# Cross-attention and a mixture of experts on one core: the expert loop of TensorE turned and lengthened, the context projection in fp32, two powers made one

## The chip, the core and the metric

The kernel runs on one core of a Trainium2 chip. The metric is device time in microseconds of one execution; the median of several executions counts. Engines: PE (TensorE), DVE (VectorE), ACT (ScalarE), POOL (GpSimd) and SP (which only issues transfers here). PE's clock is granted at one of two levels, 1.2 or 2.4 GHz (0.5 and 1.0 in the profile).

## The reference, cut to what matters

Sixteen batches (tiles) of 128 x 256. Attention part, then a mixture of 16 experts with two shared ones:

```python
def attention(x, ctx):                      # per batch: 128 x 256 each
    xn = layernorm(x)                       # over the 256 columns
    th = theta_w @ ctx + theta_b            # 64 x 256
    ph = phi_w @ xn + phi_b                 # 64 x 256
    p = softmax(th.T @ ph)                  # 256 x 256
    t = (p @ (g_w @ xn + g_b).T).T          # 64 x 256
    h = relu((t - mean(t)) * rsqrt(var(t) + 1e-5) * gamma + beta)   # mean and var of all of t
    return x + out_w @ h + out_b + ctx

def ffn(x):                                 # 2048 tokens of 256
    xt = layernorm(x)
    scores = softmax(xt @ Wg.T)             # 16 experts, 4 groups, top 2 groups, top 4 experts
    y = sum(weight[e] * (silu(xt @ W1[e].T) * (xt @ W3[e].T)) @ W2[e].T for e in chosen)
    return x + y + (silu(xt @ Ws1.T) * (xt @ Ws3.T)) @ Ws2.T
```

Inner width of an expert: 176 (2 x 176 for the shared ones).

## The kernel before, in words

Each engine runs its own program; semaphores carry every dependence, and each program's order is written out by hand.

**Attention part.** A software pipeline of `STEPS` = 21 steps. In step s each engine calls, in the order of its `step` function, the parts of tiles s, s-1, ... by lag (`tile(s, v, lag, part)`); `group(...)` parts run once for four tiles (routing: v - 8, 9 and 10; the counting matmuls and what waits for them fall into steps 10, 14 and 18). POOL's pipeline is longer (`POOL_LAG` = 11): it scatters tile s-11 into the experts' rows by four indirect DMAs a step, from step 11 on. Of the order, this matters here:

- ACT: `exps` (lag 2), `context_high` (lag 0, L499: fp16 copy of the context), copies, `theta_phi` (L458), ..., `normalised_high` (lag 0, L493: fp16 copy of the normalised x), `weights_high` (one expert's weights to fp16 a step).
- DVE: ..., `latent_var` (lag 3, L899), `stats2`, `latent_centre`, `aggr2` (lag 4, L928: `bn_aggr` of the second norm), `normalise` (lag 0, L843: first norm), `latent_out` (lag 3, L910: writes `hpre`), `weights_low` (L945), `normalise2` (lag 4, L934: writes `xn2`).
- POOL: `low` (lag 5, L1341), `context_low` (lag 1, L1315: what fp16 leaves of the context), `normalised_low` (L1335), two scatters (L1351), `latent_rstd` (lag 3, L1319: add epsilon, power -0.5, over one column), `add_context` (L1313), `rstd2` (lag 4, L1327: the same for the second norm, one column), two scatters.
- PE: `theta` (L600) and `phi` (L605) multiply high and low halves by `wparts`, three fp16 matmuls of 256 columns; `scores` (L618) uses fp32.

Matrices are kept as fp16 pairs (high, low) and three products give fp32 precision; `WS` = 64 scales the weights.

**Shared experts, first part.** `shared_units`: 11 of 16 tiles, two units a tile, while POOL finishes the scatters and DVE the last routing group.

**Expert part.** `NT` = 80 tiles of 128 rows. `expert_pipeline` runs 8 steps, then a loop of `BODY` = 8 steps a turn (nine turns), then `lags` = 3 steps. In step s:

- PE (`estep`, L778): loads addresses of four tiles' weights into registers where s % 4 == 0 (`load_four`, L353; at the turn twice, since the down matmuls still need the last ones), then transposes the hidden values of tile s-3 (L721 to L723), six up matmuls of tile s-1 (L715), five down matmuls of tile s-3 (L730).
- ACT (L561): silu of s-1 (`gate`, L528), addresses for the small transfers, fp16 copy of the hidden values of s-1 (`hidden_high`, L533), scaled copy of the result y of s-3 (L576), one small DMA (L559).
- DVE (L1257 on): copy of the transposed hidden values of s-3 (hT, L1263), low half of s-2 (L1149, L1150), product with silu of s-1 (`hidden`, L1145).
- SP loads the next rows by a transposing DMA (L421) into a ring of 8; POOL scatters y (L1378) from a ring of 4.

```python
            with eng.Fori(2 * RING, NT - BODY + 1, BODY) as i:
                for v in range(BODY):
                    if v % RING == 0:
                        r = eng.snap(4 * (i + v) + 16)
                    step(i + v, v, r)
```

**End.** The five remaining tiles of the shared experts, then SP gathers four partial results of each tile (16 loads), DVE sums them (L1278), SP stores.

Of the kernel before, what the change touches and what calls it, by code (L numbers as in the profile page):

```python
# [30 lines left out]
P = 128  # L31
B = 16
# [37 lines left out]
def build(nc, x, ctx_in, params, halves, w_in, out):  # L70
# [4 lines left out]
    with ExitStack() as stack:  # L75
# [50 lines left out]
        ctx16 = sb("ctx16", [P, 2, 2, T], F16)  # L126
# [3 lines left out]
        r1 = sb("r1", [P, B])  # L130
        xn = sb("xn", [P, 2, T])
# [14 lines left out]
        vneg = sb("vneg", [P, 2])  # L146
        vpos = sb("vpos", [P, 2])
        trs = sb("trs", [P, 2])
# [4 lines left out]
        mv2 = sb("mv2", [P, 2, 2])  # L153
        v2 = sb("v2", [P, 2])
        r2 = sb("r2", [P, 2])
# [75 lines left out]
        def pair(m):  # L231
# [15 lines left out]
                 "chi_ready clo_ready hrlo_ready xc_ready th_mm ph_mm thph_ready g_mm g_ready s_mm max_ready "  # L247
                 "p_ready pt_mm pt_ready rs_ready t_mm tx_ready ts_done ta_done tmv_ready st_mm gmv_done vneg_ready "
                 "v_done trs_ready hc_done hpre_ready ht_mm hr_ready o_mm xr_ready st2_done mv2_ready v2_done "
                 "r2_ready xn2_ready hi_ready lo_ready xt_mm xt_ready l_mm lg_ready wh_ready wl_ready "  # L250
# [17 lines left out]
        LAG = {"hlo_ready": 3, "hT_ready": 3}  # L268
# [66 lines left out]
        BODY = MR  # L335
        assert (NT - 2 * RING) % BODY == 0 and BODY % MR == 0 and NT % MR == 0 and 2 * RING == MR

        def expert_pipeline(eng, step, lags=3):


            for s in range(2 * RING):
                step(s, s, None)
            with eng.Fori(2 * RING, NT - BODY + 1, BODY) as i:
                for v in range(BODY):
                    if v % RING == 0:
                        r = eng.snap(4 * (i + v) + 16)
                    step(i + v, v, r)
            for s in range(NT, NT + lags):
                step(s, s % MR + MR, None)
# [99 lines left out]
        def _(act):  # L449
# [8 lines left out]
            def theta_phi(b, u):  # L458
# [4 lines left out]
                A(th[:, j, :], TP[0:L, 0:T], ACT.Identity, bias=c("thb", L), scale=1 / WS)  # L463
# [49 lines left out]
            def step(s, v):  # L513

                tile(s, v, 2, exps)
                tile(s, v, 0, context_high)
# [5 lines left out]
                tile(s, v, 0, normalised_high)  # L522
# [38 lines left out]
            def estep(s, step_v, r):  # L561
                v = step_v % RING
                k = (v + 1) % 2
                if has(s, 1):
                    gate(EX, s - 1, k)
                if has(s, 0) and step_v % 4 == 0:
# [3 lines left out]
                if has(s, 3):  # L570
                    t = s - 3
                    m = (step_v - 3) % YR
                    wait(act, y_out[m], 4 * (t - m))
                    act.wait_ge(meta_in[m], 4 * (t - m) + 16)
                    act.wait_ge(EX["dn_mm"], t + 1)
                    A(y_sb[:, m, :], Y[k][:, 0:T], ACT.Copy, scale=pair((step_v - 3) % MR)[0]).then_inc(EX["y_ready"], 1)  # L576
# [6 lines left out]
            expert_pipeline(act, estep)  # L583
# [4 lines left out]
        def _(pe):  # L588
# [189 lines left out]
            def estep(s, step_v, r):  # L778
# [23 lines left out]
                if has(s, 3):  # L802
# [650 lines left out]
```

## Time and profile before

| what | us |
|---|---|
| median of 3 runs | 462.05 (462.04 to 468.89) |
| the profiled execution | 459.79 |
| its span, first to last instruction | 457.8 |
| PE busy | 332.7 |
| DVE busy | 275.3 |
| POOL busy | 235.2 |
| ACT busy | 210.1 |
| mean granted PE clock | 0.818 |

The profile is of one execution, with each instruction's start and length. A matmul's end is modelled, and matmuls overlap. "Idle before" names what ended an engine's wait: an engine's instruction, a DMA, "issue" (nothing that the profile shows), or "remote" (unknown). Bracketed names such as `ctx_all` in the expert part are reused memory: `ctx_all` holds xT, y and the small transfers there.

### The profile page before, as it was taken

Reading aid. Unit: us, or ns where it says so; the run is one execution under the profiler, and the core shown is the slowest. Engines: PE = TensorE matmul, PEld = TensorE weight load, DVE = VectorE, ACT = ScalarE, POOL = GpSimd, SP = SyncE. Lnnn points to the kernel's source line nnn. Section 1 sums busy time; section 2 is a strip of 40 time slices with the busy share of each in tenths; the row PEclk is TensorE's granted clock in tenths of the full one; section 3 lists DMA queues with packets and bytes.
Section 4 is the critical chain, followed back from the end, with each engine's and each line's share of the span. In section 5 each row is a group of like instructions: output and inputs, shape, how many; then the busy total and the mean of one; then the engine's idle time right before and its main releaser. Section 6 shows DMA issues by size and latency. Waiting matters only on the chain.

```text
span 457.8 us, 9903 instructions
## 1 busy us (share of the span) xinstructions
PE 332.7 (73%) x2379; PEld 229.9 (50%) x2380; DVE 275.3 (60%) x976; ACT 210.1 (46%) x553; POOL 235.2 (51%) x284
## 2 busy tenths in 40 slices
PE   0788897977888732575099797988988798897830
PEld 0565575655566521243066465665656566574510
DVE  4488879867886883552044454555545455563686
ACT  2466765555454422331145354555555445564510
POOL 2567765588888888717500054554554445453000
PEclk9998766566555555887589999999999989999975
DMA  8713123133333342317340155555555545512994
GB/s 291 246 57 102 64 62 103 56 120 106 119 106 106 115 150 108 116 67 257 124 84 0 32 125 134 126 128 114 125 131 123 118 114 131 129 42 61 348 349 161
DMA packets 82055, 57.79 MB, mean 126 GB/s; under 512 B 58858, under 2 KB 75501, under 8 KB 82032
## 3 DMA queue, kind: packets, MB, share of 16 engines
q1 hardware_dynamic: 63600, 39.60, 30.6%
q0 software_dynamic: 6912, 17.84, 11.0%
q10 hardware_dynamic: 11520, 0.09, 1.5%
q8 instruction: 9, 0.15, 0.1%
q14 instruction: 14, 0.11, 0.1%
HBM read 24.58 MB, written 24.53 MB: 107 GB/s over the span
## 4 chain that ended last, share of the span: by engine, by line
PE 44%; POOL 17%; DVE 12%; issue 12%; another core or an unknown queue 5%; DMA 5%; ACT 2%; SPq 1%; DVEq 0%; POOLq 0%; ACTq 0%
PE bank L715 18%; PE bank L730 12%; POOL slot_rows L1351 6%; DVE x_all L1278 4%; PE bank L723 3%; POOL v L1331 3%; DMA x_all<-x_dram 3%; POOL r L1333 2%; PE bank L721 2%; DMA w<-ranked 2%; PE bank L597 2%; POOL x_all L1313 2%; PE bank L642 1%; PE bank L623 1%
## 5 line engine op out<-in xcount | busy, mean ns | idle before, releaser
L1378 POOL DMA_INDIRECT ranked<-ctx_all x80 | 79.1, 989 | 114.5 <-ACT ctx_all L576 75.4
L730 PE MATMUL bank<-w,hT 128*128 (+3 forms) x560 | 82.3, 280 | 11.2 <-DVE hT L1263 5.8
L715 PE MATMUL bank<-w,ctx_all 128*128 x480 | 85.5, 315 | 1.6 <-issue 1.3
L1351 POOL DMA_INDIRECT slot_rows<-rows_all,slot_k x64 | 65.4, 1021 | 25.6 <-issue 16.7
L1145 DVE SCALAR_TENSOR_TENSOR hid<-bank,silu 128x176 f32<-128x176 f32 x112 | 38.2, 341 | 67.1 <-ACT silu L528 42.9
L528 ACT ACTIVATE silu<-bank 128x176 f32<-128x176 f32 x112 | 35.4, 316 | 75.5 <-PE bank L715 32.2
L730 PEld LDWEIGHTS bank<-w,hT 128*128 128x128 f16 (+1 forms) x560 | 52.5, 100 | 29.9 <-issue 16.5
L533 ACT ACTIVATE hh<-hid 128x176 f16<-128x176 f32 x112 | 39.0, 348 | 39.4 <-DVE hid L1145 31.2
L721 PE MATMUL bank<-hal,hh 128*128 128x128 f16 x112 | 25.2, 225 | 41.5 <-DVE hh L1150 22.5
L715 PEld LDWEIGHTS bank<-w,ctx_all 128*128 128x128 f16 x480 | 43.0, 98 | 20.8 <-issue 3.4
L1263 DVE COPY hT<-bank 128x384 f16<-128x384 f16 x80 | 28.6, 357 | 36.7 <-PE bank L723 22.1
L721 PEld LDWEIGHTS bank<-hal,hh 128*128 128x128 f16 x112 | 11.0, 99 | 57.5 <-DVE hh L1150 27.6
L576 ACT ACTIVATE ctx_all<-bank,ctx_all 128x256 f32<-128x256 f32 x80 | 36.7, 459 | 6.2 <-PE bank L730 4.7
L715 PE MATMUL bank<-w,xT_all 128*128 128x352 f16 x192 | 37.7, 340 | 0.6 <-ACT ctx_all L576 0.6
L1149 DVE TENSOR_TENSOR hh<-hid,hh 128x48 f16<-128x48 f32 x112 | 23.0, 206 | 17.1 <-ACT hh L533 15.2
L1150 DVE TENSOR_TENSOR hh<-hid,hh 128x128 f16<-128x128 f32 x112 | 31.9, 285 | 0.4 <-issue 0.4
L623 PE MATMUL bank<-ph,th 64*128 64x256 f32 x64 | 26.7, 555 | 0.5 <-ACT ph L464 0.5
L948 DVE SCALAR_TENSOR_TENSOR w<-wst,w 128x1216 f16<-128x1216 f32 (+1 forms) x18 | 26.0, 1446 | 1.5 <-ACT w L456 1.5
L472 ACT ACTIVATE p_sb<-bank,nmax 128x256 f32<-128x256 f32 x32 | 14.9, 469 | 24.3 <-DVE nmax L865 24.3
L715 PEld LDWEIGHTS bank<-w,xT_all 128*128 (+1 forms) x192 | 19.9, 105 | 10.9 <-ACT ctx_all L576 0.9
L723 PE MATMUL bank<-hal,hh 128*128 128x128 f16 x112 | 24.8, 222 | 0.0
L722 PE MATMUL bank<-hal,hh 128*128 128x128 f16 x112 | 24.8, 221 | 0.0
(139 smaller groups left out, 607.4 us busy)
## 6 DMA issues: line engine op xcount, KB each, us to landing
wst<-w_dram SPq DMA_DIRECT2D x18, 608.0 KB
w<-ranked SPq DMA_DIRECT2D x16, 512.0 KB, 8.8
slot_rows<-pad_rows SPq DMA_DIRECT2D x17, 144.0 KB
x_all<-x_dram SPq DMA_DIRECT2D x4, 512.0 KB, 7.9
out_dram<-x_all SPq DMA_DIRECT2D x4, 512.0 KB, 4.2
ctx_all<-ctx_dram SPq DMA_DIRECT2D x1, 1536.0 KB, 10.7
ctx_all<-slot_rows SPq DMA_TRANSPOSE x80
ctx_all<-slot_rows ACTq DMA_DIRECT2D x80, 1.0 KB
```

Of the source, the lines that this page charges most:

```text
L528: A(silu[:, j, :], U[j][:, 0:NF], ACT.Silu, scale=1 / WS).then_inc(G["silu_ready"], 1)
L533: A(hh[:, j, 0:NF], hid[:, j, :], ACT.Copy).then_inc(G["hhi_ready"], 1)
L576: A(y_sb[:, m, :], Y[k][:, 0:T], ACT.Copy, scale=pair((step_v - 3) % MR)[0]).then_inc(EX["y_ready"], 1)
L623: i = mm(SP_[:, h * T:(h + 1) * T], th[:, j, h * P:(h + 1) * P], ph[:, j, :], start=True, stop=True)
L715: i = mm(U[j][:, 0:UP1], xt(2 * part + k), w[:, span(wcol + wpart * WH + k * UP1, UP1)], start=k == 0 and (wpart, part) == (0, 0), stop=k ...
L721: tr(H16[j][:, 0:P], hh[:, j, 0:FA], ident16)
L723: tr(H16[j][:, 2 * P:3 * P], hh[:, j, NF + FB:2 * NF], ident16).then_inc(done, 1)
L730: i = mm(y[:, 0:T], hT[0:rows, j, k * P:(k + 1) * P], w[0:rows, span(col, T)], start=start and n == 0, stop=stop and n == len(parts) - 1)
L1145: V.scalar_tensor_tensor(hid[:, j, :], U[j][:, NF:UP1], 1 / WS, silu[:, j, :], ALU.mult, ALU.mult).then_inc(G["h_ready"], 1)
L1150: V.tensor_tensor(hh[:, j, NF + FB:2 * NF], hid[:, j, 0:FA], hh[:, j, 0:FA], ALU.subtract).then_inc(done, by)
L1351: G.indirect_dma_start(scatter_rows, bass.IndirectOffsetOnAxis(ap=slot_k[:, b * TOPK + k:b * TOPK + k + 1], axis=0), rows32[:, b * ROW32:( ...
L1378: G.indirect_dma_start(ranked, bass.IndirectOffsetOnAxis(ap=pair(m)[1], axis=0), y_sb[:, m % YR, :], None, bounds_check=(TOPK + 1) * TOKEN ...
```

## The change

Attention part: ACT makes the first norm itself (twice, in fp16 and fp32, with scale and offset per row; POOL prepares the offset in `rstd1`). The context isn't split: one fp32 matmul. The epsilon and power of the latent norm (tile s-3) and the second norm (tile s-4) are one pair of POOL instructions over two columns, `rstd(s)`. Expert part: PE's step begins with the down matmuls of tile s-4, then transposes (s-3) and up matmuls (s-1), 24 steps a turn, with an explicit wait for y; ACT copies y of s-4 right behind silu; four steps drain instead of three.

```diff
-        LAG = {"hlo_ready": 3, "hT_ready": 3}
+        LAG = {"hlo_ready": 3, "hT_ready": 4}
...
-        BODY = MR
+        LONG = 3 * MR
...
-        def expert_pipeline(eng, step, lags=3):
+        def expert_pipeline(eng, step, lags=3, body=MR):
...
-            with eng.Fori(2 * RING, NT - BODY + 1, BODY) as i:
-                for v in range(BODY):
+            with eng.Fori(2 * RING, NT - body + 1, body) as i:
+                for v in range(body):
...
-                A(th[:, j, :], TP[0:L, 0:T], ACT.Identity, bias=c("thb", L), scale=1 / WS)
+                A(th[:, j, :], TP[0:L, 0:T], ACT.Identity, bias=c("thb", L))
...
-            def normalised_high(b, u):
-                act.wait_ge(S["xn_ready"], b + 1)
+            def normalise(b, u):
+                xs = x_all[:, span(b * T, T)]
+                by, off = r1[:, span(b, 1)], nb1[:, span(b, 1)]
+                if isinstance(b, int) and b in R1_WAITS:
+                    act.wait_ge(S["r1_done"], R1_WAITS[b])
                 wait(act, S["g_mm"], b - 1)
                 wait(act, S["ph_mm"], b - 1)
-                A(xn16[:, u % 2, 0, :], xn[:, u % 2, :], ACT.Copy).then_inc(S["xhi_ready"], 1)
-
-            def context_high(b, u):
-                if isinstance(b, int) and b in (0, 4):
-                    act.wait_ge(ctx_in_s[b // 4], 16)
-                wait(act, S["th_mm"], b - 1)
-                A(ctx16[:, u % 2, 0, :], ctx_all[:, span(b * T, T)], ACT.Copy).then_inc(S["chi_ready"], 1)
+                own_wait(act)
+                A(xn16[:, u % 2, 0, :], xs, ACT.Identity, scale=by, bias=off).then_inc(S["xhi_ready"], 1)
+                wait(act, S["xlo_ready"], b - 1)
+                own_wait(act)
+                A(xn[:, u % 2, :], xs, ACT.Identity, scale=by, bias=off).then_inc(S["xn_ready"], 1)
...
+                if has(s, 4):
+                    t = s - 4
+                    m = (step_v - 4) % YR
+                    wait(act, y_out[m], 4 * (t - m))
+                    act.wait_ge(meta_in[m], 4 * (t - m) + 16)
+                    act.wait_ge(EX["dn_mm"], t + 1)
+                    A(y_sb[:, m, :], Y[1 - k][:, 0:T], ACT.Copy, scale=pair((step_v - 4) % MR)[0]).then_inc(EX["y_ready"], 1)
                 if has(s, 0) and step_v % 4 == 0:
                     pairs.load(s, step_v)
                 if has(s, 1):
                     hidden_high(EX, s - 1, k)
-                if has(s, 3):
-                    t = s - 3
...
-            expert_pipeline(act, estep)
+            expert_pipeline(act, estep, 4)
...
             def theta(b, u):
-                pe.wait_ge(S["clo_ready"], b + 1)
+                if isinstance(b, int) and b in (0, 4):
+                    pe.wait_ge(ctx_in_s[b // 4], 16)
                 wait(pe, S["thph_ready"], b)
-                wparts(TP[0:L, 0:T], "thw", ctx16[:, u % 2, :, :]).then_inc(S["th_mm"], 1)
+                mm(TP[0:L, 0:T], c("thw"), ctx_all[:, span(b * T, T)], start=True, stop=True).then_inc(S["th_mm"], 1)
...
                     weights.load(s, step_v)
+                if has(s, 4):
+                    ready("hT_ready", 4)
+                    wait(pe, EX["y_ready"], s - 5)
+                    down(EX["dn_mm"], 1 - k, Y[1 - k], weights.of[step_v - 4], start=True, stop=True)
                 if has(s, 3):
                     ready("hlo_ready", 3)
                     transpose_hidden(EX["ht_mm"], k)
...
                     up(EX["up_mm"], k, lambda q: xT[:, m, q, :], weights.of[step_v - 1])
-                if has(s, 3):
-                    ready("hT_ready", 3)
-                    if r is None and s >= NT:
-                        pe.wait_ge(EX["y_ready"], s - 4)
-                    down(EX["dn_mm"], k, Y[k], weights.of[step_v - 3], start=True, stop=True)
-
-            expert_pipeline(pe, estep)
+
+            expert_pipeline(pe, estep, 4, LONG)
...
+                V.scalar_tensor_tensor(mvar[:, j, 2:3], gmv[:, u % 2, 0:1], gmv[:, u % 2, 0:1], gmv[:, u % 2, 1:2],
+                                       ALU.mult, ALU.subtract, reverse1=True).then_inc(S["lvar_ready"], 1)
...
-                wait(dve, S["r2_ready"], b - 1)
+                wait(dve, S["rs_done"], b)
                 own_wait(dve)
-                V.bn_aggr(mv2[:, u % 2, :], st2[:, u % 2, :]).then_inc(S["mv2_ready"], 1)
+                V.bn_aggr(mvar[:, u % 2, 0:2], st2[:, u % 2, :]).then_inc(S["mv2_ready"], 1)
...
-                G.tensor_tensor(rs, rs, c("half")[:, 0:4], ALU.pow).then_inc(S["r1_done"], 1)
+                G.tensor_tensor(rs, rs, c("half")[:, 0:4], ALU.pow).then_inc(S["r1_eps"], 1)
+                pool.wait_ge(S["r1_eps"], 3 * n + 2)
+                nb = nb1[:, 4 * n:4 * n + 4]
+                G.tensor_tensor(nb, mv1[:, 4 * n:4 * n + 4, 0:1].rearrange("p b c -> p (b c)"), rs, ALU.mult).then_inc(S["r1_eps"], 1)
+                pool.wait_ge(S["r1_eps"], 3 * n + 3)
+                G.tensor_scalar(nb, nb, -1.0, None, ALU.mult).then_inc(S["r1_done"], 1)
...
+            def rstd(s):
+                j = s % 2
+                a, z = (0 if s >= 4 else 1), (2 if s < B + 3 else 1)
+                if s < B + 3:
+                    pool.wait_ge(S["lvar_ready"], s - 2)
+                if s >= 4:
+                    pool.wait_ge(S["mv2_ready"], s - 3)
+                wait(pool, S["hpre_ready"], s - 4)
+                wait(pool, S["xn2_ready"], s - 5)
+                G.tensor_scalar(veps[:, j, a:z], mvar[:, j, 1 + a:1 + z], EPS, None, ALU.add).then_inc(S["v_done"], 1)
+                pool.wait_ge(S["v_done"], s - 2)
+                G.tensor_tensor(rs[:, j, a:z], veps[:, j, a:z], c("half")[:, a:z], ALU.pow).then_inc(S["rs_done"], 1)
...
                 tile(s, v, 5, low)
-                tile(s, v, 1, context_low)
                 tile(s, v, 1, normalised_low)
                 tile(s, v, 11, scatter[0])
                 tile(s, v, 11, scatter[1])
-                tile(s, v, 3, latent_rstd)
+                if 3 <= s < B + 4:
+                    rstd(s)
                 tile(s, v, 2, add_context)
-                tile(s, v, 4, rstd2)
```

## Rows read from the trace of the kernel before

**Rows 1.** The page, busy us (share) xcount of PE, and the queue q8

```profile
PE 332.7 (73%) x2379; PEld 229.9 (50%) x2380; DVE 275.3 (60%) x976; ACT 210.1 (46%) x553; POOL 235.2 (51%) x284
...
q8 instruction: 9, 0.15, 0.1%
```

**Rows 2.** Windows: stretch, us, busy of each engine, PEclk, DMA share, GB/s

```profile
37.15:68.74 31.59, 28.31 (x188) 19.94 (x188) 26.09 (x77) 21.75 (x53) 22.04 (x32) 0.73 0.24 79
68.74:87.75 19.01, 15.99 (x107) 12.03 (x107) 17.59 (x79) 10.84 (x28) 8.57 (x17) 0.61 0.21 67
87.75:152.33 64.58, 53.24 (x302) 37.81 (x301) 47.75 (x161) 34.10 (x80) 56.51 (x73) 0.55 0.35 118
256.90:412.10 155.20, 135.28 (x1096) 94.83 (x1097) 82.49 (x313) 81.53 (x235) 74.89 (x76) 0.99 0.50 116
```

**Rows 3.** POOL's timeline in step 12: start us, us, line, operation

```profile
99.41 0.67 POOL L1317 TENSOR_TENSOR ctx<-ctx_all,ctx 128x256 f16<-128x256 f32 x1
100.04 0.66 POOL L1337 TENSOR_TENSOR xn<-xn 128x256 f16<-128x256 f32 x1
...
103.19 0.19 POOL L1323 TENSOR_SCALAR vpos<-vneg 128x1 f32<-128x1 f32 x1
103.46 0.57 POOL L1325 TENSOR_TENSOR trs<-vpos,par 128x1 f32<-128x1 f32 x1
104.01 0.71 POOL L1313 TENSOR_TENSOR x_all<-x_all,ctx_all 128x256 f32<-128x256 f32 x1
104.81 1.49 POOL L1331 TENSOR_SCALAR v<-mv 128x1 f32<-128x1 f32 x1
...
110.13 0.67 POOL L1317 TENSOR_TENSOR ctx<-ctx_all,ctx 128x256 f16<-128x256 f32 x1
```

**Rows 4.** DVE's timeline in steps 10 and 12

```profile
83.75 0.18 DVE L932 BATCH_NORM_AGGREGATE mv<-st 128x2 f32<-128x6 f32 x1
...
84.53 0.34 DVE L915 SCALAR_TENSOR_TENSOR hpre<-tx,trs,par 128x128 f32<-128x128 f32 x1
...
104.80 1.41 DVE L948 SCALAR_TENSOR_TENSOR w<-wst,w 128x1216 f32 x1
```

**Rows 5.** Line L353: xcount, duration ns min/median/max, first and last start

```profile
L353 PEldq TENSOR_LOAD <-tab_i x30: 327/334/626, 256.2 to 411.1; - x30
```

**Rows 6.** Chain of waits, expert part: start us, us, what

```profile
277.24 1.53 issue
...
300.14 1.18 issue
...
305.08 0.90 PE bank L715 x6
305.98 0.55 PE bank L730 x5
306.52 0.06 PE bank L721
...
308.14 0.15 issue
...
308.57 1.09 PE bank L723
```

**Rows 7.** Timeline of all engines: start us, us, engine, [idle before <-releaser]

```profile
309.69 0.47 ACT L576 ACTIVATE ctx_all<-bank,ctx_all 128x256 f32<-128x256 f32 x1 [0.99 <-PE bank L730]
309.74 0.36 DVE L1263 COPY hT<-bank 128x384 f16<-128x384 f16 x1 [1.42 <-PE bank L723]
...
310.24 0.39 PE L730 MATMUL bank<-w,hT 128*128 x2 [0.68 <-DVE hT L1263]
```

**Rows 8.** POOL's power over four columns, groups view of 0 to 182 us

```profile
L1303 POOL TENSOR_TENSOR r<-r,par 128x4 f32<-128x4 f32 x4 | 4.2, 1044 | 0.3
```

**Rows 9.** Chain of waits, where step 9 passes to step 10

```profile
77.19 2.00 PE bank L623 x4
79.19 0.75 PE bank L597 x3
```

More of the change, by code:

```diff
@@ L130, in build @@
         r1 = sb("r1", [P, B])
+        nb1 = sb("nb1", [P, B])
         xn = sb("xn", [P, 2, T])
@@ L145, in build @@
         gmv = sb("gmv", [P, 2, 2])
-        vneg = sb("vneg", [P, 2])
-        vpos = sb("vpos", [P, 2])
-        trs = sb("trs", [P, 2])
+        mvar = sb("mvar", [P, 2, 3])
+        veps = sb("veps", [P, 2, 2])
+        rs = sb("rs", [P, 2, 2])
         hpre = sb("hpre", [P, 2, 2 * L])
@@ L515, in step @@
                 tile(s, v, 2, exps)
-                tile(s, v, 0, context_high)
                 tile(s, v, 5, copy_xT)
@@ L521, in step @@
                 tile(s, v, 4, high)
-                tile(s, v, 0, normalised_high)
+                tile(s, v, 0, normalise)
                 tile(s, v, 2, weights_high, count=NU)
@@ L569, in estep @@
                     hidden_high(EX, s - 1, k)
-                if has(s, 3):
-                    t = s - 3
[L572 to L576, printed above, removed]
                 if has(s, 0):
@@ L841, in _ @@
             V.scalar_tensor_tensor(small16[:, 1, :], small32, WS, small16[:, 0, :], ALU.mult, ALU.subtract).then_inc(S["small_lo"], 1)
-            def normalise(b, u):
-                j = u % 2
-                if isinstance(b, int) and b in R1_WAITS:
-                    dve.wait_ge(S["r1_done"], R1_WAITS[b])
-                wait(dve, S["xlo_ready"], b - 1)
-                V.tensor_scalar(xn[:, j, :], x_all[:, span(b * T, T)], mv1[:, span(b, 1), 0:1].rearrange("p a c -> p (a c)"),
-                                r1[:, span(b, 1)], ALU.subtract, ALU.mult).then_inc(S["xn_ready"], 1)
             def relu_low(b, u):
@@ L912, in latent_out @@
                 dve.wait_ge(S["hc_done"], b + 1)
-                dve.wait_ge(S["trs_ready"], b + 1)
+                dve.wait_ge(S["rs_done"], b + 1)
                 wait(dve, S["ht_mm"], b - 1)
-                V.scalar_tensor_tensor(hpre[:, j, :], tx[:, j, :], trs[:, j:j + 1], c("beta"), ALU.mult, ALU.add).then_inc(S["hpre_ready"], 1)
+                V.scalar_tensor_tensor(hpre[:, j, :], tx[:, j, :], rs[:, 1 - j, 1:2], c("beta"), ALU.mult, ALU.add).then_inc(S["hpre_ready"], 1)
             def residual(b, u):
@@ L929, in aggr2 @@
                 dve.wait_ge(S["st2_done"], b + 1)
-                wait(dve, S["r2_ready"], b - 1)
+                wait(dve, S["rs_done"], b)
                 own_wait(dve)
-                V.bn_aggr(mv2[:, u % 2, :], st2[:, u % 2, :]).then_inc(S["mv2_ready"], 1)
+                V.bn_aggr(mvar[:, u % 2, 0:2], st2[:, u % 2, :]).then_inc(S["mv2_ready"], 1)
             def normalise2(b, u):
                 j = u % 2
-                dve.wait_ge(S["r2_ready"], b + 1)
+                dve.wait_ge(S["rs_done"], b + 2)
                 wait(dve, S["lo_ready"], b - 1)
-                V.tensor_scalar(xn2[:, j, :], x_all[:, span(b * T, T)], mv2[:, j, 0:1], r2[:, j:j + 1],
+                V.tensor_scalar(xn2[:, j, :], x_all[:, span(b * T, T)], mvar[:, j, 0:1], rs[:, j, 0:1],
                                 ALU.subtract, ALU.mult).then_inc(S["xn2_ready"], 1)
@@ L1120, in step @@
                 group(s, v, 9, group_before)
-                tile(s, v, 0, normalise)
                 group(s, v, 10, slots_by_rank)
```

42 lines of the change are left out of this document (9 added, 33 removed).

## The prediction

> **What bounds the kernel now.** I read the page first: over the span PE is busy 332.7 us, 73% [rows 1], and no engine is full. So I cut the span into stages by the windows view [rows 2]. In the attention part at 37.2 to 68.7 us no engine fills its time. From 87.8 to 152.3 us POOL is busy 56.51 of 64.58 us, more than any other, and each step there carries four scatters. From 256.9 to 412.1 us, the expert part, PE is busy 135.28 of 155.20 us at a granted clock of 0.99. The last 45.7 us of the span (shared rest, gathers, sums) hold nothing that the change touches; they shift.
>
> The POOL timeline of one scattering step [rows 3] shows its instructions end to end from 99.41 to 110.13 us: a step of 10.72 us, and POOL is what sets it. The vector timeline of a counting step [rows 4] shows the other kind: `bn_aggr` ends at 83.93 us and `hpre` starts at 84.53.
>
> In the chain of waits of the expert part [rows 6] a tile is six up matmuls 0.90, five down 0.55 and three transposes of 0.06 each: 1.62 us. Eighty would take 130 us; the stage takes 155.2. The missing 25 come at two places in every turn of eight tiles. At the turn PE has nothing issued for 1.18 us, and its restart is 0.17 slower on the first transpose and 0.17 on the up group: 1.5 us, nine times. In the middle, where the next four weight addresses are loaded (30 register loads on PE, 327 to 626 ns [rows 5]), PE idles 0.15 us, restarts slowly, and then waits: the transposes are issued at 308.57, but their hT copy starts at 309.74 and the down group at 310.24 [rows 7], 0.9 us late against a plain tile. The timeline of the three engines [rows 7] tells more: the y copy, which needs only the down group that the chain shows ended at 308.14, also starts at 309.69. Two engines resume together, long after the PE work that they wait for. So PE's signals come late there. I count this in seven of the nine middles (and once at a turn); in two it is absent.
>
> **The change, part by part.**
>
> *POOL, the step with scatters.* The low half of the context goes: 0.63 us from start to start (99.41 to 100.04) [rows 3]. Of the two pairs (add epsilon, power) one is left. Now: 103.19 to 103.46 is 0.27, to 104.01 is 0.55, the second add without its hold-up 0.35 (it took 0.27 of work in calmer steps), the second power 0.56 as the first: 1.73. Afterwards 0.27 plus a power over two columns. No row shows that width; one column takes 0.57 [rows 3], four take 1.04 [rows 8], so it lies between; nearest to one, I take 0.72. Saved: 1.73 - 0.99 = 0.74, with the context 1.37 us. Steps 11, 12, 13, 15 and 16 go by POOL: 5 x 1.37 = 6.9. Step 17 has no context left: 0.7. Bounds of the power move this by 1.
>
> The add at 104.81 took 1.49 us; the weights' low half on DVE (1.41 us) ran from 104.80 [rows 3, 4]. So POOL stands still beside it once a step, 1.2 us longer than the add needs. The edit moves the merged pair ahead of it, and the hold-up will fall on the context add or a scatter: neither saved nor added.
>
> *The merged pair waits longer.* It needs the second norm's aggregate, and DVE's `hpre` now stands behind it, with the weights' low half and `xn2` queued behind `hpre`, and ACT's copy and POOL's `low` behind those. In a plain step the aggregate comes 2 us before POOL gets there, so nothing. In steps without scatters (3 to 8) `xn2` waited for the second power anyway: `hpre` 0.7 and weights 1.4 now follow it, as long as what is removed; zero, either end 0.3 a step. In the counting and group steps 9, 10 and 14 `hpre` could start at 84.53 [rows 4]; afterwards at 83.92 + 0.1 + 0.99 = 85.0, and what follows at the DVE is contiguous. With a little more behind it I take +0.7 each, 2 in all (bounds 0 and 4). Step 18 gives nothing.
>
> *Context in one fp32 matmul.* Two of the fp32 score matmuls with 256 columns take 2.00 us and three fp16 ones 0.75 in the same step [rows 9], in a stretch whose granted clock is 0.61 on average, so mostly at 1.2 GHz [rows 2]: +0.25 a step on PE, half of that at 2.4 GHz. POOL or DVE cover it in the scattering steps; in some six PE-bound steps it counts: +1. The context's ACT copy (16) goes; the first normalise moves from DVE to ACT, where it stands twice in place of one copy. ACT is busy 34.1 of 64.58 us [rows 2]; nothing, and DVE's removed 0.4 lay in its wait for POOL. Without that cover it would be 0.4 a step. POOL's first reciprocal gets two more instructions, four times: the first tile later by up to 0.8, behind the loads; +0.3.
>
> Attention part: -6.9 - 0.7 + 2 + 1 + 0.3 = -4.3 us.
>
> *Expert part.* The order of PE's groups stays: transposes, up, down. The boundary moves, so address loads and the turn stand behind the up group instead of the down group. The up group runs 0.90 us, and its issue is done earlier; a load of 0.33 and its 0.2 of register work then fits beside it. I take 0.1 for a middle (now 0.32 without the late signals) and 1.1 for a turn (now 1.5). Turns go from nine to three, middles from ten to sixteen: 9 x 1.5 + 10 x 0.32 = 16.7 becomes 3 x 1.1 + 16 x 0.1 = 4.9: -11.8. Bounds: 0 and 0.32 for a middle, 0.6 and 1.5 for a turn. The late signals cost 8 x 0.9, some 7 us, now. Nothing in the edit removes their cause as far as I see it (seven of nine middles, all at full pace with transposing loads and scatters under way); PE will be at full pace longer, so +1.5. On ACT y moves into the gap behind silu, where ACT waits for DVE's product; silu already starts 0.04 after its matmul, so it gains nothing while PE leads, and y lands within the two tiles that its buffer allows. PE's new wait for y is 1.4 us early for the same reason. PE gets no more idle, so I expect no change of its clock. Sum -10.3 us; with the ACT order's help in catching up after a turn I say -11.
>
> Total: the profiled execution took 459.79 us (span 457.8 and 2.0 around it). 459.8 - 4.3 - 11 = 444.5. The median is 462.05, 0.5% above that execution; so 446.5 us, rounded 446.
>
> **The rivals.**
> *A, late signals go too:* if they come from catching up after a turn, they vanish with it: another 8.5 off, 438, and 430 with a better attention part. For: two middles have none. Against: I see one before a load as well.
> *B, the place of a load doesn't matter:* a middle costs 1.2 wherever it stands. Then 6 turns become middles: 6 x 0.3 = 2 us, 446 becomes 455. For: four-tile spacing of loads is kept.
> *C, slower:* the late signals are made by a load issued while matmuls run. At turns the array stands idle during the load, and only one of nine shows them; in the middles seven of nine do. Afterwards all twenty loads run beside the up group, whose own signal, silu's start, is then late as well, with some 0.5 us of slack behind it. The worst middle now cost 2.1 us (1.53 us of missing issue at 277.24 [rows 6]). Twenty at 2.7 are 54 against 24 now: 462 - 4 + 30 = 488 at worst; over 471 from 1.9 us a load on. Against: the first loads of the stage ran beside matmuls without it.
> *D, the long body doesn't stay in the instruction memory.* The instruction queue q8 moved 9 packets of 16.7 KB in 0.1% of 16 engines' span, about 0.8 us each [rows 1]; nine for the whole program leave none for each of nine turns. A body three times as long (24 tiles of about 38 instructions) might be fetched in every turn: four packets each, of which the first is waited for, some 2 us a turn, more behind scatters: +5, 451. The Trainium skill, "Runtime: NRT & Kernel Launch", Instruction fetch mechanics, says that a taken branch to a target outside the current two-page window stalls for a fetch, and gives PE room for 2048 instructions: by that the body's 912 would stay.
> *E, attention part bounded by DVE:* the merged wait costs 1.5 us in each group step: no gain there, 451.
>
> **How the numbers follow.** Forecast 0.40, A 0.23, B 0.15, C 0.10, D 0.06, E 0.06. A measurement tells about 2% from no change (9 us). Faster: forecast, A and half of D and E, 0.68. Same, 453 to 471: B, rest, 0.23. Slower: 0.09. Range 430 to 466: A's end to a mild C.
>
> **What would show it.** Scattering steps of about 9.3 us on POOL; a gap at only two inner turns, and none at the fours; expert stage near 144 us. Wrong if middles still cost 1.2 us, if silu starts late behind each load, if PE waits on an instruction fetch at the turn, or if `hpre` waits in plain steps.

## The result, and the profile after

The changed kernel took 470.04 us (median; 469.39 to 472.04) against 462.05 us: ratio 1.018, 95% interval 1.0115 to 1.0243. It is slower; I had forecast 446, with 430 to 466 as range. Its profiled execution took 469.89 us, span 468.1 (before: 459.79, 457.8).

First the windows, over the same parts of the work as [rows 2] (columns as there):

```profile
92.25:151.35 59.10, 50.97 (x296) 34.76 (x295) 43.21 (x155) 36.69 (x81) 47.97 (x54) 0.64 0.38 121
255.30:420.90 165.60, 135.31 (x1099) 92.97 (x1100) 80.85 (x315) 80.78 (x234) 74.08 (x75) 0.99 0.49 109
```

The six scattering and counting steps take 59.1 us instead of 64.6. The expert part does the same PE work (135.31 us busy, 135.28 before, at the same granted clock of 0.99) in 10.4 us more: time in which PE waits.

To split the difference of the two spans (+10.3 us) I take four marks from the timelines: the last `low` of POOL (179.17 before, 176.96 after), and the first and last start of the 80 `hT` copies of the expert part, for after:

```profile
259.52 0.35 DVE L1252 COPY hT<-bank 128x384 f16<-128x384 f16 x1
...
423.44 0.36 DVE L1252 COPY hT<-bank 128x384 f16<-128x384 f16 x1 [0.74 <-issue]
```

Before they start at 260.04 and 415.05. So: attention part -2.2; from there to the first tile +1.7; expert part 163.9 against 155.0, +8.9; the rest +1.9. The gain of the attention part was given back on the way, and the expert part, of which I had expected -11, lost 9.

The chain of waits of the expert part after the change, to be held against [rows 6] (start us, us, what):

```profile
302.18 0.06 PE bank L719
302.24 0.06 PE bank L720
302.30 0.06 PE bank L721
302.35 0.89 PE bank L713 x6
303.25 0.55 PE bank L728 x5
303.80 0.06 PE bank L719
303.86 0.06 PE bank L720
303.91 1.05 PE bank L721
304.96 0.03 issue
...
305.14 0.37 DVE hT L1252
305.51 0.13 issue
305.64 0.72 PE bank L728 x5
```

The groups take what they took: up 0.89, down 0.55, a transpose 0.06. But the third transpose of the second tile stands in the chain with 1.05 us instead of 0.06: it was over at 303.97, and what it released began a microsecond later. No address load is near. The timeline of the same stretch:

```profile
303.18 0.98 POOL L1364 DMA_INDIRECT ranked<-ctx_all  x1 [0.33 <-issue]
...
303.91 0.32 ACT L525 ACTIVATE silu<-bank 128x176 f32<-128x176 f32 x1 [1.16 <-PE bank L713]
304.15 0.47 ACT L569 ACTIVATE ctx_all<-bank,ctx_all 128x256 f32<-128x256 f32 x1
...
305.14 0.36 DVE L1252 COPY hT<-bank 128x384 f16<-128x384 f16 x1 [0.54 <-PE bank L721]
305.31 0.32 ACT L525 ACTIVATE silu<-bank 128x176 f32<-128x176 f32 x1 [0.25 <-PE bank L713]
305.45 0.98 POOL L1364 DMA_INDIRECT ranked<-ctx_all  x1 [1.29 <-ACT ctx_all L569]
```

`silu` starts at 303.91, though its up group ended at 303.25 (0.04 after it is normal); `hT` at 305.14 instead of 304.06. This repeats along the stage: these two tiles take 4.2 us and not 3.2 (from the down group at 301.46 to the one at 305.64), and 26 of the 80 `hT` copies start over 0.9 us behind their transposes, 8 before the change. It is what I had seen before the change in seven of nine middles: signals of PE that come late. The trace also holds each change of a semaphore. Held against the modelled ends of the matmuls that raise it, 27 of 165 recorded signals of the expert part came over 0.1 us late before, 22 us in sum; after, 100 of 212, 97 us in sum. Of the 240 signals a trace records 138 to 220 in the kernels with scatters and 236 in those without, so the counts below are rough, for the kernels with y first (138 to 160 recorded) above all. And since a matmul's end is modelled, the trace can't tell a late signal from a late write of its result.

Of the kernels below, attn_ysilu, attn_dummy and late_scatter were profiled in a slow execution, so what is read from these three profiles is rough, while their ratios are taken from undisturbed ones.

### The profile page after: what moved, and what is told of

It reads as the page before. It is cut to its first block, busy times and chain, and to the rows that moved or that the text cites. A ratio compares the mean times of both kernels' runs of the same rounds, so it can differ in the third digit from the quotient of the medians.

```text
span 468.1 us, 9837 instructions
## 1 busy us (share of the span) xinstructions
PE 337.6 (72%) x2363; PEld 227.6 (49%) x2364; DVE 264.4 (56%) x960; ACT 216.1 (46%) x553; POOL 207.1 (44%) x246
## 4 chain that ended last, share of the span: by engine, by line
PE 33%; DVE 11%; another core or an unknown queue 8%; issue 6%; POOL 5%; ACT 3%; DMA 2%; POOLq 0%; ACTq 0%; SPq 0%; DVEq 0%
PE bank L713 16%; PE bank L728 11%; DVE x_all L1267 4%; PE bank L721 3%; POOL slot_rows L1338 3%; DVE hT L1252 2%; DMA w<-ranked 2%; ACT silu L525 2%; PE bank L719 1%; DVE hid L1134 1%; PE bank L720 1%; POOL rows_all L1328 1%; ACT hh L530 1%; POOL rs L1320 1%
## 5 line engine op out<-in xcount | busy, mean ns | idle before, releaser
L1338 POOL DMA_INDIRECT slot_rows<-rows_all,slot_k x64 | 70.5, 1102 | 26.4 <-issue 16.7
L728 PEld LDWEIGHTS bank<-w,hT 128*128 128x128 f16 (+1 forms) x560 | 50.1, 100 | 62.9 <-issue 51.4
L713 PE MATMUL bank<-w,xT_all 128*128 128x352 f16 x192 | 39.7, 352 | 0.6 <-issue 0.6
L640 PE MATMUL bank<-g_sb,pT 128*128 128x64 f32 x128 | 23.8, 350 | 0.4 <-ACT pT L477 0.4
```

Source lines behind the costliest of these rows:

```text
L713: i = mm(U[j][:, 0:UP1], xt(2 * part + k), w[:, span(wcol + wpart * WH + k * UP1, UP1)], start=k == 0 and (wpart, part) == (0, 0), stop=k ...
L728: i = mm(y[:, 0:T], hT[0:rows, j, k * P:(k + 1) * P], w[0:rows, span(col, T)], start=start and n == 0, stop=stop and n == len(parts) - 1)
L1338: G.indirect_dma_start(scatter_rows, bass.IndirectOffsetOnAxis(ap=slot_k[:, b * TOPK + k:b * TOPK + k + 1], axis=0), rows32[:, b * ROW32:( ...
```

## The experiments

Sixteen kernels ran. The ratio is to the kernel before, run beside them; "expert part" is first to last start of the 80 `hT` copies in the profiled run; "late" is the count and sum of signals over 0.1 us late, worked out as above.

| kernel | median us | ratio, 95% | expert part | late |
|---|---|---|---|---|
| before | 462.05 | 1 | 155.0 | 27 of 165, 22 us |
| after | 470.04 | 1.018, 1.0115 to 1.0243 | 163.9 | 100 of 212, 97 us |
| attn_only | 455.74 | 0.982, 0.9755 to 0.9878 | 154.0 | 30 of 178, 18 |
| body8 | 468.19 | 1.011, 1.0051 to 1.0168 | 164.1 | 118 of 216, 102 |
| yfirst_wait | 456.48 | 0.985, 0.9796 to 0.9896 | 152.4 | 46 of 160, 44 |
| yfirst_nowait | 454.87 | 0.981, 0.9762 to 0.9859 | 150.2 | 53 of 142, 36 |
| attn_ysilu | 464.89 | 1.001, 0.9947 to 1.0066 | 164.8 | 56 of 185, 44 |
| attn_dummy | 457.05 | 0.986, 0.9717 to 1.0005 | 158.5 | 47 of 179, 40 |
| attn_long | 460.02 | 0.995, 0.9895 to 0.9998 | 153.6 | 33 of 180, 27 |
| fixed_after | 468.68 | 1.013, 1.0024 to 1.0241 | 163.9 | 87 of 194, 96 |
| late_scatter | 463.74 | 0.990, 0.985 to 0.9958 | 160.3 | 67 of 188, 69 |
| attn_delay | 473.86 | 1.020, 1.0132 to 1.0271 | 166.4 | 81 of 207, 62 |
| no_scatter | 437.15 | 0.937, 0.9284 to 0.9462 | 132.0 | 0 of 236, 0 |
| no_scatter_before | 445.27 | 0.957, 0.9503 to 0.9637 | 143.6 | 0 of 236, 0 |
| half_rows | 467.62 | 1.008, 1.0026 to 1.0137 | 162.8 | 96 of 209, 92 |
| half_bytes | 467.29 | 1.010, 0.9971 to 1.0232 | 161.0 | 116 of 220, 97 |
| y_after_t | 455.50 | 0.987, 0.9774 to 0.9962 | 148.8 | 43 of 138, 28 |
| yfirst_scat_up | 452.88 | 0.978, 0.9681 to 0.9871 | 149.2 | 49 of 139, 28 |

The kernel before took 464.5 to 467.5 us in the median in these comparisons and 459.79 in its profile: ratios judge the time, profiles say where it goes. "Expert part" and "late" are of one execution each, and the executions of one kernel lie several us apart (attn_long: 455.11 to 461.18, its profile the shortest), so a difference of 1 to 3 us between two of these entries shows nothing by itself.

### Which part of the change

**attn_only** is the changed kernel with the five places of the expert part put back:

```diff
-        LAG = {"hlo_ready": 3, "hT_ready": 4}
+        LAG = {"hlo_ready": 3, "hT_ready": 3}
-        LONG = 3 * MR
+        LONG = MR
-            expert_pipeline(act, estep, 4)
+            expert_pipeline(act, estep)
...
```

and ACT's and PE's `estep` as before.

> The changed attention part with the expert part of before. In the profile of the changed kernel the attention part ends 2.2 us earlier than before, the expert part takes some 10 us longer. If the two parts do not touch each other: 460 us, ratio 0.995, and the expert part again 152 to 155 us. If the attention part were the culprit (its two steps of 12 us, a later start of the scatters), the time would be near the changed kernel's 470.

Measured 455.74 us and 0.982, a larger gain than the 0.995 that I expected: the attention part is the good half of the change, and the expert part the bad one. The spans of the two profiled executions differ by only 3.7 us (457.8 to 454.1), so some of the 1.8% isn't placed.

**body8** is `LONG = MR` alone.

> The changed kernel with PE's loop body back at 8 tiles, all else as changed. Theory of the issuer (PE's issue of a tile takes as long as the array; its signals are held until it has a pause; the new wait for y and the missing wait for hT take the pauses away): the late signals stay, turns add some 1 us in six places, 470 to 476 us. Theory of the long body (24 tiles a turn, its instruction fetches): 460 us or below.

Expert part 164.1, as with 24 tiles. Queue q8 moved 9 packets in this kernel and 12 with the long body, and the expert parts are equal: the long body is not the loss.

**yfirst_wait** moves ACT's y copy (lag 4 kept) ahead of `gate`. Before the change it stood behind `hidden_high`, in the changed kernel it stands between the two.

```diff
+                if has(s, 4):
+                    ...
+                    A(y_sb[:, m, :], Y[1 - k][:, 0:T], ACT.Copy, ...)
                 if has(s, 1):
                     gate(EX, s - 1, k)
-                if has(s, 4):
-                    ...
```

**yfirst_nowait** also takes PE's wait out of the loop:

```diff
-                    wait(pe, EX["y_ready"], s - 5)
+                    if r is None and s >= NT:
+                        pe.wait_ge(EX["y_ready"], s - 5)
```

> The changed kernel with ACT's y ahead of silu again, PE's wait for y kept. Theory of the issuer: PE's signals are still late in nearly every second tile, since the wait instruction is still there, but y comes earlier and PE seldom stands for it: 462 to 468. Theory of y's place (only that y behind silu reaches PE's new wait too late): the whole loss of the expert part is gone, 450 to 455, with signals on time.

> The same, and PE's wait for y taken out of the loop (with y ahead of silu the other waits order it; it stays in the last tiles). Theory of the issuer: one wait instruction a tile less, but the down group no longer stops for hT either, so late signals go down yet don't vanish: 452 to 462. Theory of y's place: as the run with the wait, within 1 us. If signals are late only behind address loads, as I predicted blind: 446 to 450.

152.4 and 150.2 us: with PE's order, its long body and its wait as changed, y's place alone brings 11.5 us back, and the ratios say the same (1.018 and 0.985, intervals apart). What the wait costs is not shown: the 2.2 us are between two single executions, and the ratios, 0.985 and 0.981, overlap. Neither theory had it quite: signals still come late, but the long delays are rarer (8 and 7 `hT` copies over 0.9 us behind their transposes, 26 after the change).

**attn_ysilu** is the reverse, on attn_only: y behind silu, with the old lag and the old order on PE.

> The changed attention part, the expert part of before, and in it only ACT's y moved behind silu (same tile, same lag, PE as before). In the earlier runs this part alone took 154 us with y ahead of silu. If y's place alone costs the 11 us (it makes y land too late whatever PE does): 465 us or more, expert part 163. If it costs only together with the down group at the head of PE's step and its wait for y: 456 us as the run it is built on, within 3.

164.8 us, and no gain left in the time (1.001, its interval apart from that of attn_only). So y behind silu costs some 10 us under either order of PE, and not through PE's wait for y, which this kernel lacks. But here it moves y the other way: without the longer lag y comes earlier than behind `hh`, not later. One tile, whose down group ends at 278.17:

```profile
277.46 0.71 PE L728 MATMUL bank<-w,hT 128*128 x5
278.29 0.48 ACT L569 ACTIVATE ctx_all<-bank,ctx_all 128x256 f32<-128x256 f32 x1 [0.19 <-PE bank L728]
...
279.58 0.98 POOL L1365 DMA_INDIRECT ranked<-ctx_all  x1 [0.63 <-issue]
```

The scatter starts 1.4 us behind the down group, against 1.74 in attn_only; the 2.6 us that the expectation of attn_delay below gives for y behind silu holds for the changed kernel only.

**attn_long** is attn_only with `expert_pipeline(pe, estep, 3, LONG)` and `LONG = 3 * MR`.

> The changed attention part and the expert part of before, with PE's loop body at 24 tiles. Six turns of 1.5 us become middles of some 1.2: 2 us less, 454. If a long body costs fetches: 458 or more. In the changed kernel the long body against 8 tiles made no gain (470.0 against 468.2).

The profile says no cost (153.6), the ratio 0.995 says that it isn't better than attn_only at 0.982. The long body brings nothing here; whether it costs something in the average execution stays open.

### What holds the signals: PE's issue?

My theory at that point was that PE's issue is full and that a signal waits for a pause in it. Two kernels: one more wait on PE that is always passed, on attn_only, and constant addresses in the changed kernel (all tiles with the first expert's weights), which takes the register instruction away from each matmul.

```diff
                     ready("hT_ready", 3)
+                    wait(pe, EX["up_mm"], s - 5)
```
```diff
-                    up(EX["up_mm"], k, lambda q: xT[:, m, q, :], weights.of[step_v - 1])
+                    up(EX["up_mm"], k, lambda q: xT[:, m, q, :], 2 * WU)
```

and the same for `down`.

> The changed attention part and the expert part of before, with one more wait instruction a tile on PE that is always passed already (an old up group), 0.05 us in PE's issuer. Theory of the issuer (a tile's issue is as long as the array's 1.61 us, and signals are held while the issuer has no pause): pace 1.65 us a tile or late signals outside the address loads, 460 us or more. If issue has room: no change, 455 to 457.

> The changed kernel with constant weight addresses in all up and down groups of the expert part (every tile computes with the first expert's weights; the address loads stay), which takes the register instruction before each matmul away, 11 of 0.046 us and their share of issue a tile. Theory of the issuer: PE's issuer gets pauses back, late signals become rare outside the loads, the expert part falls from 164 us to 140 or less, time under 450. Theory of y's place alone: the two-tile rhythm and its late signals stay, 465 or more.

attn_dummy took 457.05 us where the theory wanted 460 or more, but is unclear in itself (0.986, 0.9717 to 1.0005). fixed_after decides: 163.9 us and 87 late signals with an issuer that has 11 instructions a tile less. The theory of the issuer falls.

### What holds them: POOL's scatter

What stood beside the late signals was a scatter: in the changed kernel 27 of 41 down groups that ended 0.5 to 1.25 us behind the start of one were late, none of 14 at less than 0.5. That window holds for these down groups alone: of the up groups of the same kernel 17 of 23 were late that ended within 0.25 us of a scatter's start, and of the 27 late signals before the change 14 belong to groups that ended 1.25 to 1.5 us behind one. Common to the kernels is only that most late signals belong to groups that ended within 1.5 us: before 26 (of 92 recorded there) and 1 farther off (of 76), after 87 (of 161) and 12 farther off (of 54). And most arrive once the scatter's instruction of 0.98 us is over: after the change 85 of 99 came 1.25 to 2.5 us behind its start.

y sets the scatter: it starts 0.82 us after y ends (304.62 to 305.45 above). In the changed kernel, with y behind silu and one tile later, that is 2.6 us behind the tile's own down group where nothing is late (1.31 to y, 0.47 for it, 0.82), against 1.75 before. For some of the kernels, over all 80 scatters, counted from the end of the tile's own down group (median; the lowest tenth in brackets) and from the end of the latest down group of any tile (median):

| kernel | from its own, us | from the latest, us | expert part |
|---|---|---|---|
| before, attn_only | 1.74 (1.58) | 0.22 | 155.0, 154.0 |
| yfirst_wait | 2.36 (2.10) | 0.61 | 152.4 |
| yfirst_nowait | 2.45 (2.15) | 0.73 | 150.2 |
| yfirst_scat_up | 2.56 (2.11) | 0.82 | 149.2 |
| y_after_t | 2.63 (2.19) | 0.85 | 148.8 |
| after, body8 | 3.4 (2.60) | 1.00 | 163.9, 164.0 |
| attn_delay | 3.52 (2.62) | 1.10 | 166.4 |
| late_scatter | 3.07 (3.00) | 1.38 | 160.3 |
| attn_ysilu | 1.41 (1.33) | 1.39 | 164.8 |

By the second distance the kernels fall into two sets, up to 0.85 us and from 1.0 on, and the expert part goes with it. That is an ordering found in the traces: late signals shift the distances too, and no run sets this one by itself. The next kernels test whether it is the scatter at all. **no_scatter** replaces the expert tiles' scatter:

```diff
-                G.indirect_dma_start(ranked, ...).then_inc(y_out[m % YR], 16)
+                pool.sem_inc(y_out[m % YR], 16)
```

and the last loads read `x`; **no_scatter_before** does so on attn_only.

> The changed kernel with the expert tiles' scatters left out (POOL only counts the semaphore up; the last loads read x in place of the scattered rows, as many bytes). Theory of the collision: hardly a late signal from PE, the expert part falls from 164 us to 140 or less. If the late signals come from SP's transposing loads or from PE's own waits: 160 or more.

> The same with the expert part of before (on the changed attention part): scatters left out. Theory of the collision: the late signals behind PE's address loads, 0.9 us in seven of nine middles, go too; expert part 154 down to 140 to 146. If they are made by the address loads themselves: 152 or more.

Not one late signal in either, of 236. The grouped lines of the `hT` copies from 262 to 380 us count the tiles of those 118 us; no_scatter, then no_scatter_before, then after, then before (xcount | busy, mean ns | idle before, releasers):

```profile
L1252 DVE COPY hT<-bank 128x384 f16<-128x384 f16 x71 | 25.4, 358 | 12.2 <-PE bank L721 7.9
```
```profile
L1253 DVE COPY hT<-bank 128x384 f16<-128x384 f16 x65 | 23.3, 358 | 18.6 <-PE bank L721 15.5
```
```profile
L1252 DVE COPY hT<-bank 128x384 f16<-128x384 f16 x56 | 20.0, 356 | 21.5 <-remote 7.2 <-PE bank L721 6.3 <-issue 5.4
```
```profile
L1263 DVE COPY hT<-bank 128x384 f16<-128x384 f16 x60 | 21.4, 357 | 29.1 <-PE bank L723 17.5 <-issue 6.7 <-remote 2.3
```

71 tiles are 1.66 us each, PE's own pace of 1.62 but for the turns; 65 are 1.82, 60 are 1.97, 56 are 2.11. The chain of no_scatter, to be held against that of after: nothing but PE groups.

```profile
300.46 0.90 PE bank L713 x6
301.36 0.61 PE bank L728 x5
301.97 0.06 PE bank L719
302.03 0.06 PE bank L720
302.09 0.06 PE bank L721
302.14 0.90 PE bank L713 x6
```

The address loads are still in both kernels. So they don't make signals late by themselves. That they shift PE against a scatter that is already due would explain why late signals stood behind them before the change; no run tested it.

Does the *place* of the scatter matter, with all else alone? **attn_delay** (on attn_only) lets POOL wait for `h_ready` of tile t+4; **late_scatter** (on the changed kernel) for `hhi_ready` of tile t+4:

```diff
                 pool.wait_ge(EX["y_ready"], t + 1)
+                if not isinstance(t, int) or t + 4 <= NT:
+                    pool.wait_ge(EX["h_ready"], t + 4)
```

(the last eight tiles are written out of the loop, since the count ends there).

> The changed attention part and the expert part of before, in which only POOL's scatter of tile t also waits for DVE's hid of tile t+4, which puts it 2.6 us behind its down group instead of 1.75, where y behind silu puts it too; y, ACT, DVE and PE are as before. Theory of the collision: signals of the down group and the transposes late in many tiles, expert part 160 us or more against 154, time 462 or more. Theory of y's place alone: a scatter has slack (its buffer comes round after four tiles), no change, 455 to 457.

> The changed kernel, in which POOL's scatter of tile t also waits for ACT's hh of tile t+4 and so starts some 0.4 us or more later after y. Theory of the collision (PE's signals come late when they fall into some 0.2 to 1.0 us after the start of a scatter; y behind silu has put the scatter of one tile, 2.7 us behind its down group, onto the down group and the transposes of the next, 0.5 to 0.7 us into it): the scatter now starts 3.1 us behind its down group, at the next but one, the late signals go down by more than half, and a kernel with one wait more is faster: expert part 150 to 156 us, 455 to 462. Theory of y's place alone (y too late for PE's wait): another wait can only cost, 470 or more.

attn_delay touches POOL alone, and the expert part goes from 154.0 to 166.4 us (ratio 1.020 against 0.982, intervals apart): as much as y behind silu costs. A scatter that ends later frees its buffer of y later, but that isn't the price: from 262 to 380 us ACT stands 0.0 us idle ahead of its y copies. A stretch of its chain of waits shows the same sign as the changed kernel's:

```profile
288.02 0.55 PE bank L728 x5
...
288.68 1.22 PE bank L721
...
290.48 0.72 PE bank L728 x5
```

late_scatter adds a wait to the changed kernel and makes it faster, 0.990 against 1.018, intervals apart. Only part of the gain that I expected: 160.3 us instead of 150 to 156, and 67 late signals instead of fewer than 50. Why the rest didn't come is not shown; stalls that shift PE against the scatters again would do it.

What of a scatter does it? **half_rows** places 64 of the 128 rows, **half_bytes** half of each row (both on the changed kernel, the last loads read `x`):

```diff
-                G.indirect_dma_start(ranked, bass.IndirectOffsetOnAxis(ap=pair(m)[1], axis=0),
-                                     y_sb[:, m % YR, :], None, ...)
+                G.indirect_dma_start(ranked, bass.IndirectOffsetOnAxis(ap=pair(m)[1][0:64], axis=0),
+                                     y_sb[0:64, m % YR, :], None, ...)
```

> The changed kernel, in which each expert tile's scatter places only 64 of its 128 rows (half the descriptors, half the bytes; the last loads read x). If making or moving a scatter's descriptors is what holds PE's signals, late signals fall by a third or more and the expert part goes from 164 us to 140 to 155; if it is the scatter as an instruction on POOL, whatever its size, 160 to 165.

> The same with all 128 rows but half of each row (as many descriptors, half the bytes). Bytes as the cause: as half_rows or better. Descriptors as the cause: as the changed kernel, 160 to 165 us in the expert part.

162.8 and 161.0 us against 163.9, 96 and 116 late signals against 100: the cost doesn't shrink with the descriptors or the bytes. The instruction itself hardly gets shorter with half the rows either, 929 ns against 987 (993 with half the bytes), which fits a cost of the instruction as such; a shorter one was not tried:

```profile
L1364 POOL DMA_INDIRECT ranked<-ctx_all x57 | 52.9, 929 | 105.9 <-ACT ctx_all L569 88.1 <-issue 17.8
```

(half_rows, groups view, POOL, 262 to 380 us.) How a scatter holds up PE's signals, the trace doesn't show.

Last, two kernels that move the scatter in yfirst_nowait: **y_after_t** lets y wait for the next transposes as well (`act.wait_ge(EX["ht_mm"], s - 2)`), **yfirst_scat_up** lets POOL wait for `up_mm` of tile t+4.

> The kernel with y ahead of silu and no wait in the loop (454.9 us), with y of tile t also waiting for the transposes of tile t+1, which puts y and its scatter 0.2 us later: the scatter starts 1.5 us behind its down group instead of 1.33, nearer to the 1.75 of before, where signals fall just ahead of it. Theory of the collision: fewer late signals than 53 of 142, expert part 145 to 150 us. If the place of a scatter makes no such difference: 0.2 us a tile can't help, 150 to 153.

> The same kernel, in which only the scatter waits, for the up group of tile t+3: it starts some 1.95 us behind its down group. Theory of the collision: between the best place and the worst (2.6); by the phases of the earlier runs the up group's signal is then 0.7 us into a scatter and the other two 1.3 to 1.5: 148 to 158 us in the expert part. I can't say better; the run maps the phase.

148.8 and 149.2 against 150.2: small, and in the time not to be told from it. Their phases aren't those that the expectations took: the scatters of yfirst_nowait, y_after_t and yfirst_scat_up start 2.45, 2.63 and 2.56 us behind their own down group in the median, not 1.33, 1.5 and 1.95, since ACT reaches y later than the down group's end. So these two runs map little; they show that such small shifts bring nothing clear. yfirst_scat_up has the lowest median of all kernels that compute the whole, 452.88, ratio 0.978 (0.9681 to 0.9871): the version to keep, though attn_only and the three with y first lie within each other's intervals.

## Why the prediction was wrong

**The step that failed** is one sentence on ACT: "y moves into the gap behind silu", costed at nothing because ACT had the gap and y "lands within the two tiles that its buffer allows". As far as these waits go it holds: no_scatter has y in that place and PE's wait for it, and its tiles take 1.61 us. But y sets off POOL's scatter, and the scatter's start, moved from 1.75 to 2.6 us and more behind the down group, fell where PE's signals come late. Price: 10 to 12 us of the expert part (after to yfirst_wait 11.5; by the scatter alone, moved as far on the old order, attn_delay, 12.4; moved 0.3 us the other way, attn_only to attn_ysilu, 10.8). I had asked what a moved step waits for, and not what it triggers.

**The term mis-sized** is the late signals. I had seen them, counted 7 us, and wrote "nothing in the edit removes their cause as far as I see it", +1.5. They rose from 22 to 97 us in sum. I tied them to the address loads, because they stood there; a scatter that had begun at most 1.5 us earlier stood beside 26 of those 27 too. Without scatters and with all loads there is none.

**What was right and didn't show.** For turns and middles I had worked out -11.8. Between the two kernels without scatters it is 143.6 to 132.0, -11.6, and not by luck: from the starts of the `hT` copies a turn there costs 1.39 us and a middle 0.37 in the old order (I had 1.5 and 0.32), 1.07 to 1.14 and 0.05 to 0.23 in the new (1.1 and 0.1). With the scatters and y first, 4 to 5 of it are left (155.0 or 154.0 to 150.2). PE's new wait for y, which I took as free, is free in no_scatter; beside scatters the profiles differ by 2.2 (152.4 to 150.2), which two executions don't show.

**Attention part**, forecast -4.3: the last `low` starts at 179.17 before; in attn_only at 174.54 (-4.6), after the change at 176.96 (-2.2), and the first `low` already differs by as much from run to run (36.3 and 38.1, 37.15 before). So attn_only's -4.6 is near the forecast partly by luck: from the first `low` to the last it is -3.8, after the change -3.1. By steps (from `low` to `low`, after against before): the five scattering steps without a count take 46.7 us instead of 53.9, -7.2 where I had -6.9; step 17 -1.3 instead of -0.7. The counting and group steps 9, 10 and 14 lost 1.4, 1.7 and 1.7 us, where I had +0.7 each; steps 5 to 8 together, where I had put the fp32 context matmul and next to nothing for the merged wait, lost 0.55. POOL in step 14 after the change:

```profile
123.56 0.96 POOL L1338 DMA_INDIRECT slot_rows<-rows_all,slot_k  x1 [0.30 <-issue]
127.46 0.24 POOL L1318 TENSOR_SCALAR veps<-mvar 128x2 f32<-128x2 f32 x1 [2.93 <-issue]
127.78 0.72 POOL L1320 TENSOR_TENSOR rs<-veps,par 128x2 f32<-128x2 f32 x1
```

and DVE:

```profile
127.14 0.17 DVE L922 BATCH_NORM_AGGREGATE mvar<-st 128x2 f32<-128x6 f32 x1
127.23 0.39 DVE L1072 TENSOR_TENSOR onek<-onek,slot 128x256 f32<-128x256 f32 x1
128.59 0.77 DVE L905 SCALAR_TENSOR_TENSOR hpre<-tx,rs,par 128x128 f32<-128x128 f32 x1 [0.97 <-issue]
```

POOL, which has less to do and gets there earlier, stands 2.93 us idle for the aggregate, and `hpre` stands behind it: the wait that I had priced at 0.7 is the largest of the step. The power over two columns took the 0.72 that I had chosen.

**The rivals.** C had the sign, and the late signals as its means, but not the place: it put them behind address loads, and they come in tiles without one. D: body8's expert part is no shorter, and of the 12 code packets after the change (9 before) none comes between 314.9 and 435.1 us, while the second and third turn run. By the 2048 instructions that the Trainium skill, "Runtime: NRT & Kernel Launch", Instruction fetch mechanics, gives PE, the body would stay in its memory; the trace agrees with that. The stall for a branch out of a two-page window, which the same section has too and which a body of four packets should have met at each turn, doesn't show. E holds for three steps: 1.4 to 1.7 us each, near its 1.5; the plain steps went by POOL as forecast. A had the late signals vanish, and they do only without scatters. B, a middle that costs as much wherever it stands, falls with the 0.37 and the 0.05 to 0.23 us of the kernels without scatters.

## What to carry to other kernels

Before moving a step off the critical path, list what it sets off (here a scatter on another engine) and put the start of that beside the signals of the engine that bounds, moved earlier as well as later; a step with slack of its own can still move a collision. If two engines resume together long after the work that they wait for, look at what every other engine was doing at that time, and take that away in one run: leaving the scatter out told in one run what three theories about PE had not. And a gain that doesn't show may still be there: the same change was worth 11.6 us as soon as the collision was gone.

## What the runs showed of the hardware

Beside indirect scatters on POOL, signals of TensorE come late (27 of 165 recorded before, 100 of 212 after the change, none of 236 without the scatters), 26 of the 27 and 87 of some 100 of them of groups that ended within 1.5 us behind a scatter's start, and most arrive after its 0.98 us are over; in the changed kernel by up to 1.33 us with no address load near (a down group's, at 313.28). Which groups in that stretch are hit differs from kernel to kernel; with 80 scatters of 0.98 us in the expert part that costs 10.4 us in the order of before (154.0 to 143.6) and 31.9 in that of the change (163.9 to 132.0). Moving the scatters alone costs 12.4 us (attn_delay). Half the rows or half the bytes change it little (162.8 and 161.0 against 163.9). Why a scatter does this is open.

The shared part has a similar sign, ACT standing 17.6 us from 208.63 on while the last scatters of the attention part are issued one after the other (15.1 and 2.8 us from 209.81 on before the change); that the scatters are its cause was not tried. In the chain of waits of after it stands as:

```profile
208.63 17.58 another core or an unknown queue
226.23 0.33 ACT silu L525
```
